# Attention on one core: the value products of two key tiles issued together in every second unit

## The reference, cut to what matters

```python
q = (x @ Wq + bq).reshape(b, n, H, HD)
k = (x @ Wk + bk).reshape(b, n, H, HD)
v = (x @ Wv + bv).reshape(b, n, H, HD)
scores = jnp.einsum('bqhd,bkhd->bhqk', q, k) / jnp.sqrt(jnp.float32(HD))
scores = scores + (1.0 - adj)[None, None, :, :] * -1000000000.0
attn = jax.nn.softmax(scores, axis=-1)
out = jnp.einsum('bhqk,bkhd->bqhd', attn, v).reshape(b, n, d)
return out @ Wo + bo
```

## Time and profile before

| | |
|---|---|
| median of the runs | 3125.32 us |
| span of the profiled execution, first to last instruction | 3120.2 us |
| granted TensorE clock, mean | 0.988 |
| TensorE matmul busy | 3039.6 us (97%) |
| TensorE weight loads busy | 2162.3 us (69%) |
| VectorE busy | 2430.3 us (78%) |
| ScalarE busy | 2135.5 us (68%) |
| GpSimd busy | 590.0 us (19%) |

### The profile page before, as it was taken

One profiled execution on the slowest core, in us unless ns is written; L12 is line 12 of the kernel. 1 busy time (PEld: TensorE's weight loads), 2 busy tenths in 40 slices (PEclk: granted clock), 3 DMA queues, 4 the chain that ended last, 5 costly groups with the idle time before them and its releaser, 6 DMA issues.

```text
span 3120.2 us, 64907 instructions
## 1 busy us (share of the span) xinstructions
PE 3039.6 (97%) x23872; PEld 2162.3 (69%) x23872; DVE 2430.3 (78%) x4427; ACT 2135.5 (68%) x3794; POOL 590.0 (19%) x538
## 2 busy tenths in 40 slices
PE   7999997999999999999999999999999999999999
PEld 6888886667666666666676667676767666666666
DVE  6776766888787878787878888877778787878776
ACT  3000005888787878787778777887878787878887
POOL 2222220114040405050413223010101010102000
PEclk9999998999999999999999999999999999999999
DMA  3101104232222323233223242323232222323232
GB/s 118 48 17 46 55 14 104 55 82 69 73 66 72 80 53 89 62 76 70 71 62 89 77 113 62 89 62 89 62 86 65 69 69 60 91 52 85 65 72 55
DMA packets 123648, 217.86 MB, mean 70 GB/s; under 512 B 20017, under 2 KB 88241, under 8 KB 123313
## 3 DMA queue, kind: packets, MB, share of 16 engines
q1 hardware_dynamic: 122160, 209.14, 27.0%
q0 software_dynamic: 1152, 4.19, 0.4%
HBM read 53.87 MB, written 25.17 MB: 25 GB/s over the span
## 4 chain that ended last, share of the span: by engine, by line
PE 82%; issue 1%; DVE 1%; DMA 0%; ACT 0%; POOL 0%; DVEq 0%; ACTq 0%; POOLq 0%
PE t_pt_ps L739 34%; PE t_ot_ps L758 19%; PE t_s_ps L727 15%; PE t_g_ps L713 4%; PE t_g_ps L712 4%; PE t_g_ps L714 4%; PE t_g_ps L779 1%; PE t_g_ps L783 1%; PE t_g_ps L798 1%; DMA mask<-in_adj 0%; DVE t_T L945 0%; DVE t_w_lo L1045 0%; ACT t_T L876 0%; PE t_pt_ps L712 0%; PE t_pt_ps L714 0%
## 5 line engine op out<-in xcount | busy, mean ns | idle before, releaser
L945 DVE CUSTOM_DVE_ANT_0 t_T<-t_s_ps,mask 128x1024 f32<-128x1024 f32 x1024 | 1246.0, 1217 | 237.9 <-PE t_s_ps L727 230.2
L876 ACT ACTIVATE t_T<-t_T,t_low 128x1024 f32<-128x1024 f32 x1024 | 1177.8, 1150 | 54.7 <-DVE t_low L945 40.5
L739 PEld LDWEIGHTS t_pt_ps<-t_ident,t_T 128*128 128x128 f32 x8192 | 887.8, 142 | 434.4 <-issue 389.3
L739 PE MATMUL t_pt_ps<-t_ident,t_T 128*128 128x128 f32 x8192 | 1132.0, 282 | 7.5 <-DVE t_PT L1020 6.3
L881 ACT ACTIVATE t_PT<-t_pt_ps 128x512 f32<-128x512 f32 x1324 | 757.8, 596 | 427.0 <-PE t_pt_ps L739 426.6
L727 PE MATMUL t_s_ps<-t_k,t_q 128*128 128x512 f32 x2048 | 737.1, 441 | 34.3 <-issue 30.3
L758 PE MATMUL t_ot_ps<-t_PT,shared 128*32 128x256 f32 x8192 | 658.4, 394 | 0.3 <-ACT t_PT L881 0.2
L1020 DVE COPY t_PT<-t_pt_ps 128x512 f32<-128x512 f32 x724 | 500.1, 691 | 175.0 <-PE t_pt_ps L739 162.2
L758 PEld LDWEIGHTS t_ot_ps<-t_PT,shared 128*32 128x32 f32 x8192 | 162.6, 108 | 311.9 <-issue 274.2
L727 PEld LDWEIGHTS t_s_ps<-t_k,t_q 128*128 128x128 f32 x2048 | 313.6, 194 | 37.4 <-issue 34.2
L255 ACT ACTIVATE g_yT_hi<-g_ps 128x512 fp32r<-128x512 f32 x64 | 38.3, 598 | 401.1 <-PE g_ps L195 401.1
(11 more groups left out here) (185 smaller groups left out, 3160.6 us busy)
## 6 DMA issues: line engine op xcount, KB each, us to landing
t_q<-t_st_hi SPq DMA_DIRECT2D x256, 128.0 KB, 2.3
t_k<-t_st_hi SPq DMA_DIRECT2D x256, 128.0 KB, 2.4
t_k<-t_st_lo SPq DMA_DIRECT2D x256, 128.0 KB, 2.4
t_q<-t_st_lo SPq DMA_DIRECT2D x256, 128.0 KB, 2.4
shared<-x_after_graph_layers SPq DMA_DIRECT2D x8, 1024.0 KB, 8.0
t_xe<-x_after_graph_layers SPq DMA_DIRECT2D x32, 256.0 KB, 3.7
x_after_layer<-t_xe SPq DMA_DIRECT2D x32, 256.0 KB, 2.2
shared<-x_after_layer SPq DMA_DIRECT2D x8, 1024.0 KB, 6.5
```

Of the source, the lines that this page charges most:

```text
L739: last = nc.tensor.transpose(pt_ps[half][:, i * P:(i + 1) * P], T[u % RING][:, kt * P:(kt + 1) * P], ident[:])
L876: nc.scalar.activation(T[u % RING][:], T[u % RING][:], ACT.Exp, bias=low[:, u % RING:u % RING + 1], scale=-1.0, accum_out=rsum[:, u:u + 1] ...
L945: nc.vector.tensor_tensor_reduce(out=T[u % RING][:], in0=s_ps[u % 2][:], in1=mask[:, qt, :], scale=1.0, scalar=3.4e38, op0=ALU.add, op1=AL ...
```

## The change

TensorE's value products are issued in even units only, for the key tile of that unit and of the next, and in odd units not at all. ScalarE's copy of `ot_ps` is written with the same constant; with `GROUP = 2` it falls into the same units and waits for the same count as before. Nothing else is changed.

```diff
 UNITS = 64
+GROUP = 2
...
-                    if u >= NT or before is not None:
-                        values(job, u)
+                    if u % GROUP == 0 and (u >= NT or before is not None):
+                        for w in range(u, u + GROUP):
+                            values(job, w)
                     transposes(job, u)
...
-                    if u % (2 * NT) == NT - 1 and (u >= NT or before is not None):
-                        copy_ot(UNITS * job + u + 1 - NT)
+                    if u % (2 * NT) == NT - GROUP + 1 and (u >= NT or before is not None):
+                        copy_ot(UNITS * job + u + GROUP - 1 - NT)
```

## The result

The changed kernel takes 3033.8 us in the median of 4 runs (3030.82 to 3034.35), the kernel before 3124.88 us (4 runs). The ratio is 0.9711, 95% interval 0.9699 to 0.9724: 2.9% faster, 91 us. The forecast was 3018 us, with a range of 2978 to 3062. By the spans of the two profiled executions the gain is 88.5 us (3120.2 to 3031.7).

What follows compares the result with a forecast made beforehand. TensorE's own instruction sequence was taken to bound the kernel. 143 us gross less 26 and 10 gave 107 off the 3120.2 us span, 3013, plus 5.1 outside the span: 3018 us, range 2978 to 3062.

Steps and rivals of the forecast that it cites:

- (d): Releases coming one key tile early or late, and loads of q and k under 7% shorter pairs: cost nothing.
- The bound: Whole kernel: TensorE's own sequence sets the time, as long as the copies keep up; TensorE busy 97% of the span.
- 3.85 + 0.08 of the forecast: Plain pair of units: 3.85 us by TensorE's own intervals, plus 0.08 us lost waiting for VectorE's copy.
- The gross gain: Value products: two groups at 0.716 become one at 0.716 plus 0.434, saving 0.282 us in 508 pairs, 143 us.
- (a): Odd units without a block: second-half transposes wait for VectorE's copy, about 0.08 us in 311 units, 26 us given back.
- Two signs that I named: Some hundreds of 0.1 us waits of TensorE's transposes for VectorE's copy; VectorE's share up from 78% to 81%.
- (b): VectorE's 3.66 us and ScalarE's 3.24 to 3.72 us of work fit a 3.85 us pair; no cost by themselves.
- rival 2: Units without values: copies become the bound, each odd unit without a block gives back 0.37 us, 3107 us; chance 0.10.
- the 1.83 of my sum: VectorE's time in us for one masking and one copy, in a unit without value products.
- (c): Unit 8: value products wait about 0.5 us for ScalarE's copy of finished products; 0.6 a job, 10 us given back.
- the forecast's 107: Net gain in us off the profiled span of 3120.2 us: 143 - 26 - 10.
- the 5.1 us between the span and the median of the kernel before: Median 3125.3 against span 3120.2 us, put down to what lies around the span and added to the forecast.

Runs made afterwards that it cites:

- experiment 1: Changed kernel, but even units issue one key tile's value products ahead of the transposes and the other's behind them: 3150.6 us, ratio 1.0094 to the kernel before.
- experiments 3 and 4: Changed kernel with copies of transposes cut to 256 of 512 columns, on VectorE alone, then on ScalarE too: 3026.3 us, then 2994.4 us.
- Experiment 2: Changed kernel with GROUP = 4 in place of 2, so four key tiles in every fourth unit: 3112.7 us, ratio 0.9965 to the kernel before.
- experiments 7 and 8: Kernel before, then changed kernel, each with its 16 jobs written out in place of hardware loops: 3074.2 us, then 2975.1 us.

## Why the prediction was right, step by step

The time lies in the range and the mechanism of the gain was as forecast. The median came 16 us above the forecast of 3018, because the sum left out three losses; they stand at (d) and behind it.

- **The bound.** TensorE's own sequence, right. Every plain pair ran at 3.93 us, which is 3.85 + 0.08 of the forecast.
- **The gross gain, 143 us.** Right. Pairs with a block in their odd unit gave 0.29, and experiment 1, with the changes of width kept, gave none of it.
- **(a) Odd units, 26 us.** Size right: 0.087 us in 244 plain pairs is 21 us, and nearly 27 with those at the other places. Cause half right. The forecast had VectorE's copy alone; the first half's wait for ScalarE's copy, 0.11 us from the copy's end to TensorE's load where I had 0.05 from the VectorE row, takes the larger part, and experiments 3 and 4 show it. Two signs that I named did not come: the profile lists 3 waits of transposes for VectorE's copy and not some hundreds, the waits being too short for it, and VectorE's share is 79% and not 81%.
- **(b) VectorE and ScalarE fit.** Right for groups of two. Experiment 2 shows how near the edge was: at four the copies are the bound, so rival 2 is real, one step further on. A unit at that bound takes 1.74 us, not the 1.83 of my sum, because a copy starts before the recorded end of the masking ahead of it (at 1331.89 and 1331.96 in that trace); so VectorE had 0.37 us left per pair, not 0.2.
- **(c) Unit 8, 10 us.** Right: the products of unit 8 started 5.09 us after the scores of unit 6 (5.07 forecast). In 15 jobs this pair has a block in its odd unit and should have gained 0.29; it lost 0.21, so 0.50 each. With unit 40's 0.09 in 15 jobs, and 0.52 in job 15, where no block hides it, that makes 9 us.
- **(d) Moved releases, put at nothing.** This step failed. It asked who waits for the value products, not what they had covered. The products of odd units had also been the time in which ScalarE and VectorE emptied the block bank. Without them unit 54 waits: 0.5 us beyond the plain loss in 15 jobs, 8 us. It also held that pairs shorter by 7% leave the loads of q and k their time. That is so within a layer, but not between the two: the 3.15 us wait in job 7, of which 2 us stay lost.
- **A term that is missing: the loop ends.** The sum gave every pair the same gain. At ten loop ends TensorE stands still, and the stalls were dearer for the body that ran faster: 10 us by the trace, 8 by experiments 7 and 8.

By the trace, 144 (508 x 0.284) - 27 - 9 - 8 - 2 - 10 = 88 us, against 88.5 between the spans. The terms that I had not seen, 20 us, are what separates the forecast's 107 from that; the forecast's own terms came within 1 us of what it gave them. I also laid the 5.1 us between the span and the median of the kernel before to what lies around the span. In the runs on record the time is 1.8 us above the span; by that the other 3.3 us say that the profiled execution was a quick one, which is why the spans give a smaller gain than the medians (88.5 us against 91).

Why a loop end got dearer is not settled. DMA carries instructions during the stall, and it is busy for 0.69 of it; that the arrival of instructions is tied to time rather than to progress would explain it, and so would a DMA made busier by other transfers, but no run here separates the two. The speed of the body alone does not set the price: experiments 3 and 4, with faster bodies still, lose 5.5 us per loop end, less than the 6.2 of the changed kernel and more than the 5.1 of the kernel before.

## What to carry to other kernels

Where float32 products of 32 columns alternate with full-width ones on TensorE, try putting several of the narrow groups together: each change there and back cost 0.28 us here, which no busy share shows, and the price stands in the start-to-start times of a place that has several groups in a row. How many to put together is set by the copies, which see the same work in a more uneven rhythm: two paid, four gave nearly all back. When work is moved away from a place, list what it had covered there (a shared bank, a queue, a late start, a DMA), and before an instruction with a wait is moved ahead, list what stands behind it.

## What the hardware showed that I had not expected

- A hardware loop's jump back cost 5.1 us of TensorE's time per iteration before the change and 6.2 after it by the traces (5.1 and 5.9 by the runs without loops), in the changed kernel with 0.50 of the clock for 3 us behind the stall. Written out, the same 16 jobs ran without these stalls and with a mean granted clock of 0.995 in place of 0.988, although the program is longer.
- In experiment 1, where one of the two narrow groups is followed by scores instead of transposes, each pair cost 0.03 us more than before, with the same number of changes of width. Which part of the pair takes it was not separated.
- A transpose's load started 0.11 us behind the end of ScalarE's copy in odd units, and 0.05 behind VectorE's. This is not a matter of the engine alone: the value products of unit 8 started 0.05 us behind the end of ScalarE's copy (1466.72 + 0.60, then 1467.37). What makes the 0.11 was not tested.
